# Expert convolutions and a gated patch filter: w_in as a stage of its own, w_out of one image among the set matmuls of the next, later gate steps

## The reference

```
gn(v): per channel, (v - mean) / sqrt(var + eps) over its pixels
x = x + experts(gn(x))    # gate: top 3 of 6 experts by image, from max + mean of each channel;
                          # expert: 3x3 depthwise conv, bias, relu, 3x3 depthwise conv, bias
x = x + filter(gn(x))     # h = w_in (170 x 32) @ x;  8x8 patches: rfft2 * filter, irfft2;
                          # y = 3x3 depthwise conv(h);  gelu(y[:85]) * y[85:];  w_out (32 x 85) @ that
```

## Time and profile before

| what | us |
|---|---|
| median of 3 runs | 3443.94 |
| lowest and highest run | 3439.81, 3449.4 |
| span of the profiled execution | 3457.4 |
| first w_in matmul of image 0 | 1182.2 |
| first w_in matmul of image 1 | 1250.1 |
| first w_in matmul of image 31 | 3362.3 |

### The profile page before, as it was taken

One profiled execution on the slowest core, in us unless ns is written; L12 is line 12 of the kernel. 1 busy time (PEld: TensorE's weight loads), 2 busy tenths in 40 slices (PEclk: granted clock), 3 DMA queues, 4 the chain that ended last, 5 costly groups with the idle time before them and its releaser, 6 DMA issues.

```text
span 3457.4 us, 164388 instructions
## 1 busy us (share of the span) xinstructions
PE 2908.9 (84%) x74374; PEld 2020.6 (58%) x74374; DVE 1847.5 (53%) x4198; ACT 1311.5 (38%) x2217; POOL 253.1 (7%) x274
## 2 busy tenths in 40 slices
PE   4699999999996788888888888888888888888887
PEld 4355554555453666666666666666656666666665
DVE  3356565565652245554556555655555555555555
ACT  1234444444342233343434343433433333443332
POOL 2011111111110200000000000000000000000000
PEclk9899999999998599999999999999998999999999
DMA  6578778787764334334443444334433444334433
GB/s 126 124 170 172 164 169 170 172 171 165 165 144 69 32 100 111 95 93 104 117 106 89 107 119 105 89 99 105 116 97 89 105 115 112 89 99 113 113 92 84
DMA packets 451958, 404.16 MB, mean 117 GB/s; under 512 B 404172, under 2 KB 404478, under 8 KB 447497
## 3 DMA queue, kind: packets, MB, share of 16 engines
q1 hardware_dynamic: 446030, 376.93, 47.5%
q10 hardware_dynamic: 5228, 16.70, 1.4%
HBM read 165.77 MB, written 78.16 MB: 71 GB/s over the span
## 4 chain that ended last, share of the span: by engine, by line
PE 49%; DVE 6%; issue 5%; ACT 3%; DMA 3%; ACTq 2%; SPq 1%; POOL 0%; DVEq 0%; POOLq 0%
PE ps L1295 12%; PE ps L1245 10%; PE ps L1280 10%; PE ps L1309 9%; PE ps L1263 8%; DMA neighbours<-border 3%; DVE gated L1356 3%; ACT gelu L1180 2%; DVE channels_first L1369 2%; ACTq L1190 2%; ACT hidden_patches L1153 1%; DVE border L1163 1%; SPq L1052 1%; ACT border L1163 0%; DMA x_normed<-in_L_conv_w_in_dram 0%
## 5 line engine op out<-in xcount | busy, mean ns | idle before, releaser
L1356 DVE TENSOR_TENSOR gated<-gelu,ps 128x432 f32<-128x432 f32 (+1 forms) x512 | 289.3, 567 | 555.8 <-ACT gelu L1180 529.7
L449 ACT ACTIVATE hidden<-ps,hidden_scale 128x576 f32<-128x576 f32 x512 | 351.7, 738 | 614.5 <-PE ps L554 614.5
L1369 DVE STREAM_TRANSPOSE channels_first<-gated 128x512 f32<-128x512 f32 x576 | 571.3, 1043 | 1.1
L1153 ACT COPY hidden_patches<-ps 128x704 f32<-128x704 f32 x576 | 406.5, 749 | 434.3 <-PE ps L1245 434.2
L1280 PE MATMUL ps<-hidden_patches,channel_tables 64*64 64x144 f32 x11264 | 403.4, 287 | 97.4 <-DVE gated L1356 97.4
L1263 PE MATMUL ps<-hidden_patches,channel_tables 64*64 64x144 f32 x11264 | 405.7, 287 | 90.2 <-DVE border L1163 84.8
L568 PE MATMUL ps<-hidden,taps 128*32 128x288 f32 x6144 | 437.3, 417 | 43.1 <-DMA taps<-conv_tables 29.7
L1245 PE MATMUL ps<-w_in_t,x_normed 32*64 32x88 f32 x18432 | 422.3, 259 | 54.2 <-issue 49.3
L1263 PEld LDWEIGHTS ps<-hidden_patches,channel_tables 64*64 64x64 f32 x11264 | 359.4, 134 | 184.6 <-ACT border L1163 114.7
L1163 ACT COPY border<-ps 128x432 f32<-128x432 f32 (+1 forms) x512 | 226.4, 495 | 618.9 <-DVE border L1163 216.9
L554 PE MATMUL ps<-x_rows,taps 32*64 32x288 f32 x12288 | 455.0, 415 | 2.5 <-issue 1.3
(11 more groups left out here) (147 smaller groups left out, 1328.7 us busy)
## 6 DMA issues: line engine op xcount, KB each, us to landing
neighbours<-border SPq DMA_DIRECT2D x1024, 126.8 KB
taps<-conv_tables SPq DMA_DIRECT2D x192, 216.0 KB
x_image<-in_x_dram SPq DMA_DIRECT2D x128, 288.0 KB, 5.8
x<-x_image SPq DMA_DIRECT2D x128, 288.0 KB, 4.7
x_image<-x SPq DMA_DIRECT2D x384, 96.0 KB
out_dram<-x_image SPq DMA_DIRECT2D x384, 96.0 KB, 2.0
x_rows<-in_x_dram SPq DMA_DIRECT2D x512, 60.0 KB
neighbours<-border ACTq DMA_DIRECT2D x1024, 15.8 KB
```

Source lines behind the costliest of these rows:

```text
L449: A(hid[T % 3][:, 2 * h:2 * h + 2, :, 1:1 + W], ps1[:, 2 * h:2 * h + 2, 0:XB * W].rearrange("p c (k w) -> p c k w", k=XB), ACT.Relu, scale ...
L1153: nc.scalar.copy(o, i).then_inc(s_we[pair], 1)
L1356: TT(o, gl[odd][:, 0:n * NPC].rearrange("p (t m) -> p t m", m=NPC), ps[:, 2 * odd + 1, 0:n * NPC].rearrange("p (t m) -> p t m", m=NPC), AL ...
L1369: last = nc.vector.transpose(t[:, s], g)
```

## The change

Part 2. The w stage makes w_in alone: a step takes all four quadrants in turn, the steps alternate between banks 4 to 7 and 0 to 3, and its 18 copies go 12 to ACT and 6 to DVE. The steps of w_out of the image before stand among the set stage's matmuls, by the list `W_OUT`: the first between the two halves of border(S+1) at the image's start, then one each in the sets 0, 3, 4 and 5 and two each in the sets 1 and 2. For that `gated` is doubled, and the transposed values lie in `x1_normed`, which is free by then; so the first transposes of an image wait for the next image's w_in. `border` comes in two halves, each into banks 6 and 7, so the second half waits until the first is copied; ACT makes nearly all of these copies (DVE two per image). PE's order in a set is add_neighbours(S), first half of border(S+2), w_out, second half, hidden(S+1). The four corner DMAs of the sets 2 to 7 go from ACT to SP; ACT keeps those of the sets 0 and 1. Stores of the image before follow at s = 2, 4, 6, loads at s = 3, 5, 7, and POOL normalises by thirds as they land. After the last image nine w_out steps follow.

Part 1. The gate steps come one or two sets later, the maximum gets the sets u = 2 and u = 5 for itself, and the 16 matmuls of `biases` become one on 48 rows, from tables that ACT loads at the start (six small DMAs more than before).

The core of the diff; of lines that only go away, most are left out, as are edits to names and tables.

```diff
+                for e in range(E):
+                    gdma(b2s[J * e:J * e + J, :], b2[e].rearrange("(f j) -> j f", f=Q))
+                gdma(own_j[:, :, :], own_c.ap().rearrange("p (j b) -> p j b", j=J))
...
-                MM(pgB[0:E, 20:20 + GB], cofe[:, :], ident[0:GB, 0:GB], start=True, stop=True).then_inc(s_gp, 1)
+                MM(pgB[0:E * J, 20:20 + GB], cofw[:, :, :].rearrange("p e j -> p (e j)"), ident[0:GB, 0:GB],
+                   start=True, stop=True).then_inc(s_gp, 1)
             def biases(g):
+                pe.wait_ge(s_b2, 1)
                 pe.wait_ge(s_gd, gate_at(g, "cofeT"))
-                for j in range(J):
-                    last = MM(pgB[:, 96 + GB * j:96 + GB * j + GB], b2x[:, j].rearrange("p f r -> p (f r)"), cofT[:, :],
-                              start=True, stop=True)
-                last.then_inc(s_gp, 1)
+                MM(pgB[:, 96:96 + J * GB], b2x[:, :, :].rearrange("p f r -> p (f r)"),
+                   cofT[:, :, :].rearrange("p j b -> p (j b)"), start=True, stop=True).then_inc(s_gp, 1)
...
-                    if u == 6:
+                    if u == 7:
                         moments(g + 1)
-                    if u == 8:
+                    if u == 9:
                         logits(g + 1)
                         row_scales(g + 1)
-                    if u == 12:
+                    if u == 14:
                         scales(g + 1)
-                    if u == 13:
+                    if u == 15:
                         biases(g + 1)
...
+            def x_max(n):
+                dve.wait_ge(s_xr[n % NXR], (n // NXR + 1) * 16 * Q)
+                if n >= GB and n % GB == 0:
+                    dve.wait_ge(s_gp, pe_at(n // GB - 1, "moments"))
+                o = n % GB * J
+                RED(mxx[:, o:o + J], xres[n % NXR][:, :, :], axis=AX.X, op=ALU.max).then_inc(s_mx, 1)
...
-                    if u in (0, 1):
-                        x_stats(2 * g + 2, u % 2 * 4, u % 2 * 4 + 4)
-                    if u in (3, 4):
-                        x_stats(2 * g + 3, (u - 3) * 4, (u - 3) * 4 + 4)
-                    if u == 6:
+                    if u in (0, 1, 3, 4):
+                        n2, part = 2 * g + 2 + u // 3, u % 3
+                        x_stats(n2, part * 4, part * 4 + 4)
+                    if u in (2, 5):
+                        x_max(2 * g + 2 + u // 3)
...
+        gts = [sb(f"gated{i}", [P, NT4, NPC]) for i in range(2)]
...
-        ct = [sb(f"channels_first{i}", [P, 2 * 512]) for i in range(2)]
...
+        ct = [xn[:, 1024 * i:1024 * i + 1024] for i in range(2)]
...
+        W_OUT = [[0], [1], [2, 3], [4, 5], [6], [7], [8], [], [], []]
+        BANK_IN, BANK_OUT, BANK_EDGE = (4, 0), 4, 6
+        VEC_PAIRS = range(1, 2 * NW, 3)
+        ACT_PAIRS = [p for p in range(2 * NW) if p not in VEC_PAIRS]
...
+                if S % NSETS >= 2:
+                    for j in range(4):
+                        f, r = EDGE + CORNER_SHIFT[j], 8 * j + 4
+                        sp.dma_start(bd[b][r:P:NV, :], be[b][r:P:NV, f:f + RUN]).then_inc(s_bc[b], 16)
...
+                move(NSETS * k)
+                move(NSETS * k + 1)
                 for s in range(NSETS):
+                    if s + 2 < NSETS:
+                        move(NSETS * k + s + 2)
+                    if k > 0 and s in (2, 4, 6):
+                        store(k - 1, (s - 2) // 2)
+                    if k > 0 and k + 1 < B and s in (3, 5, 7):
+                        load(k + 1, (s - 3) // 2)
...
                 o = xn.rearrange("p (k c r w) -> p k c r w", k=3, r=T8, c=NPR)
                 i = xr[k % 2].rearrange("p (k r c w) -> p k c r w", k=3, r=T8, c=NPR)
+                need(pool, s_w, 2 * NW * k)
+                need(pool, s_wo, NW * (k - 1))
                 for r in range(3):
-                    last = nc.gpsimd.tensor_scalar(o[:, r], i[:, r], nrm[:, k, 0:1], nrm[:, k, 1:2], ALU.mult, ALU.add)
-                last.then_inc(s_xn, 1)
+                    pool.wait_ge(s_xr[k % 2][r], (k // 2 + 1) * 16 * NQUAD)
+                    nc.gpsimd.tensor_scalar(o[:, r], i[:, r], nrm[:, k, 0:1], nrm[:, k, 1:2], ALU.mult, ALU.add).then_inc(s_xn, 1)
...
+            def edges(S, odd):
+                for y in range(2 if S % NSETS else 1):
+                    border_copy(act, nc.scalar.copy, S, odd, y).then_inc(s_pe[0], 1)
+            for k in range(B):
+                for p in ACT_PAIRS:
+                    w_in_copy(act, nc.scalar.copy, k, p).then_inc(s_we[0], 1)
+                S = NSETS * k
+                edges(S, 0)
+                edges(S, 1)
+                move_corners(S)
+                edges(S + 1, 0)
+                edges(S + 1, 1)
+                move_corners(S + 1)
+                for s in range(NSETS):
+                    gelu(S + s, 0)
+                    gelu(S + s, 1)
+                    if s + 2 < NSETS:
+                        edges(S + s + 2, 0)
+                        edges(S + s + 2, 1)
...
+            def w_in_step(k, v):
+                pe.wait_ge(s_xn, 3 * k + v // 3 + 1)
+                if v >= 2:
+                    w_in_copied(pe, k, 2 * (v - 2) + 1)
+                if v == 0:
+                    need(pe, s_r, NW * (k - 1))
+                    if k > 0:
+                        border_copied(pe, 2 * NSETS * k - 1)
+                if v == 1:
+                    need(pe, s_m, 2 * NSETS * k)
                 if k == 0 and v == 0:
+                    for h in range(2):
+                        pe.wait_ge(s_xe[h], NGX)
+                bank = BANK_IN[v % 2]
                 for i in range(WSTEP):
+                    for q in range(NQUAD):
                         cq = slice(C * q, C * q + C)
                         for h in range(2):
+                            last = MM(ps[half(h), bank + q, i * NCH:(i + 1) * NCH], xn[cq, (WSTEP * v + i) * NV:(WSTEP * v + i + 1) * NV], wi[cq, NCH * h:NCH * h + NCH],
                                       start=True, stop=True)
+                        if i == WSTEP - 1 and q % 2 == 1:
+                            last.then_inc(s_w, 1)
...
+                for m in range(CUT[s], CUT[s + 1]):
+                    o = (m - CUT[s]) * NPC
+                    for y in range(2):
+                        j = NT4 * y + 2 * m + odd
+                        for h in range(2):
+                            last = MM(ps[half(h ^ y), BANK_EDGE + y, o:o + NPC], tbl[half(h), j, NV:2 * NV], U[half(h), j, :],
+                                      start=True, stop=True)
                 last.then_inc(s_p, 1)
...
+            for k in range(B):
                 for v in range(NW):
+                    w_in_step(k, v)
+                S = NSETS * k
+                outs = W_OUT if k > 0 else [[]] * len(W_OUT)
+                border(S, 0)
+                border(S, 1)
+                hidden(S)
+                border(S + 1, 0)
+                for v in outs[0]:
+                    w_out_step(k - 1, v)
+                border(S + 1, 1)
+                for s in range(NSETS):
+                    add_neighbours(S + s)
+                    if s + 2 < NSETS:
+                        border(S + s + 2, 0)
+                    for v in outs[s + 1][:1]:
                         w_out_step(k - 1, v)
+                    if s + 2 < NSETS:
+                        border(S + s + 2, 1)
+                    for v in outs[s + 1][1:]:
+                        w_out_step(k - 1, v)
+                    if s + 1 < NSETS:
+                        hidden(S + s + 1)
+            for v in range(NW):
+                w_out_step(B - 1, v)
...
+                    dve.wait_ge(s_w, 2 * NW * min(k + 2, B))
...
+            for k in range(B):
+                for p in VEC_PAIRS:
+                    w_in_copy(dve, TC, k, p).then_inc(s_we[1], 1)
+                S = NSETS * k
+                outs = W_OUT if k > 0 else [[]] * len(W_OUT)
+                border_copy(dve, TC, S, 0, 1).then_inc(s_pe[1], 1)
+                border_copy(dve, TC, S, 1, 1).then_inc(s_pe[1], 1)
+                for v in outs[0] + outs[1]:
+                    transposes(k - 1, v)
+                for s in range(NSETS):
+                    gate(S + s, 0)
+                    gate(S + s, 1)
+                    for v in (outs[0] if s == 0 else []) + outs[s + 1][:1]:
+                        residual(k - 1, v)
+                    for v in outs[s + 2][:1]:
                         transposes(k - 1, v)
+                    for v in outs[s + 1][1:]:
+                        residual(k - 1, v)
+                    for v in outs[s + 2][1:]:
+                        transposes(k - 1, v)
+            for v in range(NW):
+                transposes(B - 1, v)
+                if v > 0:
+                    residual(B - 1, v - 1)
+            residual(B - 1, NW - 1)
```

(62 more changed lines are left out.)

141 lines of the change are left out of this document (45 added, 96 removed).

## The result

The changed kernel takes 3631.06 us in the median (3623.56 to 3641.24) against 3446.67 in the runs beside it: ratio 1.0555, 95% interval 1.053 to 1.0581. It is slower by some 184 us; 3579 had been forecast, with a range of 3320 to 3690. Its profiled execution has a span of 3621.6 us.

The account below looks back on a forecast made before the run. PE bounds the kernel, its w stage also by DVE and instruction fetch. An image takes 15.1 + 58.6 + 1.2 = 74.9 us against 70.4, times 31 = +140, less 5 for part 1: 3579 us, range 3320 to 3690.

Parts of the forecast that it names:

- The w stage: Part 2, w_in alone: bound by instruction fetch, 15.1 us an image (11.8 to 18.0).
- the price of a packet: w_in on PE: 3.67 us for each 16 KB packet of instructions where nothing hides its fetch.
- the packet in hand: Start of the w stage: 0.8 of 4.6 packets taken as already fetched, so not charged.
- SP's queue: Part 2 sets: corners queued on SP ask 7.1 us a set against PE's 6.1, stretching 52 us to 58.6.
- The wait for the third load: w_in step 6: third load normalised by 66 us, needed at 68, so its wait is hidden by 2 us.
- The set stage on PE: Part 2 sets: 52 us by PE alone, 58.6 (56.4 to 60.3) with the waits for SP.
- The clock: Part 2, each image: +1.2 us (0 to 3) for a lower clock, where it was 2.3 before.
- The last rival: Clock low through the w stage: w_in takes 21.6 us, 80.2 an image, time 3743; chance 8%.
- Image 0: First image of part 2: changes by about a microsecond, with opposite sign to the w_out steps at the end.
- Part 1: First part: -5 us (ends -65 and +10), as PE's savings mostly lengthen the first conv2's wait for second taps.
- the 8 us taken off for a lower clock: Part 1: taken from the first half's gain of 13 us, for a lower clock in a longer wait.
- The rivals that ended faster: Part 2: SP no limit, 3374, chance 16%; neither SP nor fetch a limit, 3272, chance 9%.

Follow-up runs that it names:

- half of w_in: Changed kernel with one of two column halves of each quadrant's w_in matmuls left out, copies kept; 3446.59 us, ratio 0.9978.
- little idle work: Changed kernel with corners of sets 2 to 7 on ACT, one filler matmul a w_in step and one ahead of each of the last two adds; 3511.70 us.
- the run without both: Changed kernel with corners of sets 2 to 7 on ACT and half of the w_in matmuls left out; 3341.48 us, ratio 0.9665.
- much idle work: Changed kernel with 18 filler matmuls an image in w_in and two ahead of each of the last two adds; 3744.35 us, ratio 1.0835.

## Why the prediction was right, point by point

The range, 3320 to 3690, took in a faster kernel as well, so that the time lies in it says little. The mechanisms can be checked one by one.

**The w stage: right, with its cause.** 15.1 predicted, 16.2 measured. The stops lie one packet apart, as read from the earlier trace rows, and the price of a packet was right: over the 30 images the packet boundaries lie 3.58 us apart in the mean, for 3.67. The missing microsecond is at the stage's two ends. PE takes 1.3 us for the 67 pairs of the packet in hand (half a packet, not 0.8) and 1.3 for the pairs behind the last boundary. The sum had put both at nothing, and charged 3.8 packets at the full price where 3.5 were paid. Images 0 and 25 show the cause without a doubt about the clock: 16.70 us at 1.00 with PE busy 9.35, 16.90 at 0.50 with PE busy 13.83. Halving the instructions brought the stage to 11.6, next to the 11.8 that the prediction had worked out for the copies. So the rule that the fetch is mostly hidden ("Runtime: NRT & Kernel Launch", section "Instruction fetch mechanics", of the Trainium skill) doesn't hold in this stage: 102.3 us of waits show the fetch, 17.4 with half the instructions.

**SP's queue: the right mechanism, a term too large.** The adds wait where they were said to (0.45, 2.04 and 1.59 at the last three, for 1.05 and 2.0 at the first two of these). But an issue costs 0.56 us where ACT issues little (sides 2.41 and corners 2.06 for four each), the lower end, not 0.61. And with the corners on ACT the set stage is 56.4, not 52: the term was put at 6.6 us an image, and the move gives back 3.3, net of what ACT then costs. The runs with the corners moved, all or half, forward or back, agree: -100, -50, +109 us. The wait for the third load, said to be hidden by 2 us, is 3.2 us in all after, and 21.5 with half of w_in. The Trainium skill's sentence that issuing on several engines saves only the time to issue, usually small beside the DMA ("DMA: Bandwidth & Descriptors", section "Issuing engines are not separate DMA queues"), is right of one issue here, 0.56 us beside a landing of 2.6, and misses what these three runs show, where up to twelve issues of a set stand in line.

**The set stage on PE: too short by what the clock and ACT took.** 58.6 was predicted and 59.7 measured, but by errors that cancel: SP 3.3 less than thought, the clock some 1.5 more, and 2.9 that the sum on PE had not (with little idle work and the corners on ACT, 54.9 remain where 52 was the sum). The first add was expected at 8.2 us and comes at 10.4; at clocks of 0.89 it comes at 9.6, so about half of the 2.9 lies ahead of it. In the run with little idle work PE waits 43.0 us for ACT's border copies and 40.7 for gates; how much of the rest is theirs is not shown.

**The clock: a term of the sum that was mis-sized, in place and size.** +1.2 had been allowed in all. It costs nothing that I can show in the w stage, where the next packet comes late at either clock (images 0 and 25), and about 1.6 us in the sets. Among the images 1 to 31 the stages at 0.93 and above take 14.8 to 15.6 us and those at 0.70 and below 16.7 to 18.2; whether the clock makes the wait there or the wait the clock is not shown. The last rival had feared 21.6 us of w_in at the low clock, as in image 0 before. Image 25 had the low clock and took 16.9: its price came from four tiles in turn, and the new step has eight.

**Image 0 and the end.** Image 0 was put at one microsecond and costs 5.8. It has no w_out, and the step that failed is to have charged SP's queue and the halved border only where w_out stands between: its set stage grows from 46.3 to 56.9 us all the same, while its w stage falls by 4.9. At the end, 4.4 for 3.5.

**Part 1: right.** -5 with the argument that the first conv2 would wait instead; the measured change can't be told from none, and the wait stands in the trace. That it is for the second taps is not shown: the profile names no releaser, and the 8 us taken off for a lower clock show in no run (0.98 from 187 to 1035 in both kernels).

**The sum.** An image costs 75.85 us where 74.9 was said: 31 x 0.95 = 29 us; image 0 makes 5 more, and the two profiled executions against their medians 23, with part 1 the other way. The rivals that ended faster fall for one reason each: SP's queue is a limit, the fetch is one, and only the run without both was faster.

What stays open is the last 3 us between 54.9 and 52 in the set stage (ACT's copies, its corner issues ahead of the gelus and the late first add are candidates, none tried alone), and why the clock falls at the ends of the sets where PE is busy 5.75 of 8.40 us and not in the stretch before, where it is busy 15.99 of 18.60.

## What to carry to other kernels

Before small instructions are gathered into a stage of their own, count them in packets of the instruction queue and price the packets with a stop in the trace; a mixed stage may have been hiding them. Before issues are moved to another queue, add up that queue by set, the shortest sets included: 128 of the 177 us of waits stood at the last two. Where PE is freed ahead of a step that waits for something else, look whether the wait only moves, as it did in part 1.

## What the runs showed of the hardware that was not expected

- Four DMAs of a third of an image as one: the issue stays at 0.53 to 0.58 us, but its packets ran about four at a time instead of up to 16 (DMA share 0.24), a load was of use 6.9 us after its issue began, and SP's queue stood 10 us behind a store.
- A w_in stage with much idle work is bistable: 19.7 us at clock 1.00, or 31.5 at 0.50 throughout, though PE is busy 95 to 97% in both.
- Eight tiles in turn instead of four gain more at the low clock than at the full one: 127 pairs in 2.21 us where 64 took 1.24 at 1.00, that is 17 and 19 ns a pair; at 0.50, 127 in 3.06 (image 25) where 64 took 2.12 in image 0 before, 24 and 33 ns. The end of the last one is included in all four. The row of image 0 before:

```profile
1184.55 2.12 PE L1245 MATMUL ps<-w_in_t,x_normed 32*64 32x88 f32 x64 [0.19 <-ACT hidden_patches L1153]
```

- Where PE stood for instructions it resumed 1.39 us (median) after their packet had been moved, and the packet boundaries lay 3.6 us apart at a clock of 0.50 (image 25), as in the mean of all images.
